# A GRU recurrence inside a graph network: one hand-over of the new state instead of two, gate sums in SBUF instead of PSUM

## The reference, cut to what matters

```python
def step(h, pi):                     # pi: what the input gives to the gates, computed ahead
    ph = h @ W_hh.T + b_hh           # 512 -> 1536
    r = sigmoid(pi[:H] + ph[:H])
    z = sigmoid(pi[H:2*H] + ph[H:2*H])
    n = tanh(pi[2*H:] + r * ph[2*H:])
    h_new = (1.0 - z) * n + z * h
    return h_new, h_new
ys = scan(step, h0, pre_i)           # 1250 steps, each needs the state of the one before
```

## Time and profile before

| | |
|---|---|
| median of 3 runs | 5284.1 us (5284.08 to 5288.26) |
| the profiled execution's own time | 5288.3 us, its span 5286.2 us |
| PE busy | 5071.3 us, 96% of the span |
| PE weight loads | 4262.3 us, 81% |
| DVE, ACT, POOL busy | 57%, 40%, 18% |
| matmuls of the recurrence (L501) | 120000 of 128234 |

### The profile page before, as it was taken

One profiled execution on the slowest core, in us unless ns is written; L12 is line 12 of the kernel. 1 busy time (PEld: TensorE's weight loads), 2 busy tenths in 40 slices (PEclk: granted clock), 3 DMA queues, 4 the chain that ended last, 5 costly groups with the idle time before them and its releaser, 6 DMA issues.

```text
span 5286.2 us, 338777 instructions
## 1 busy us (share of the span) xinstructions
PE 5071.3 (96%) x128234; PEld 4262.3 (81%) x128235; DVE 3006.4 (57%) x16450; ACT 2112.3 (40%) x15422; POOL 943.4 (18%) x5221
## 2 busy tenths in 40 slices
PE   5669999999999999999999999999999999999989
PEld 4555559999999999999999999999999645555654
DVE  6662336666666666666666666666666444355551
ACT  0110005555555555555555555555555201221110
POOL 1230002222222222222222222222222100000000
PEclk8559999999999999999999999999999998999989
DMA  1002220000000000000000000000000100001011
GB/s 59 0 3 97 80 87 0 0 0 0 0 0 0 0 0 0 0 0 0 0 0 0 0 0 0 0 0 0 0 0 0 54 8 10 35 35 35 19 46 45
DMA packets 28930, 81.07 MB, mean 15 GB/s; under 512 B 1594, under 2 KB 1834, under 8 KB 28858
## 3 DMA queue, kind: packets, MB, share of 16 engines
q1 hardware_dynamic: 28858, 80.03, 4.1%
HBM read 58.08 MB, written 21.95 MB: 15 GB/s over the span
## 4 chain that ended last, share of the span: by engine, by line
PE 92%; DVE 3%; issue 3%; DVEq 2%; ACT 0%; POOL 0%; DMA 0%; SPq 0%; POOLq 0%; ACTq 0%
PE psum L501 63%; PE psum L570 8%; PE psum L376 5%; PE psum L366 4%; PE psum L582 4%; PE psum L483 2%; PE psum L556 2%; PE psum L646 1%; PE psum L423 1%; DVE r L879 1%; DVEq L874 1%; DVE r L878 1%; DVEq L872 1%; DVEq L871 1%; PE psum L433 0%
## 5 line engine op out<-in xcount | busy, mean ns | idle before, releaser
L501 PE MATMUL psum<-h,r 128*128 128x16 f16 (+1 forms) x80000 | 3063.4, 181 | 11.1 <-ACT psum L706 4.4
L501 PEld LDWEIGHTS psum<-h,r 128*128 128x128 f16 x80000 | 2544.2, 96 | 113.0 <-ACT psum L706 5.0
L501 PE MATMUL psum<-h,hn 128*128 128x16 f16 (+1 forms) x40000 | 1801.3, 178 | 0.0
L501 PEld LDWEIGHTS psum<-h,hn 128*128 128x128 f16 x40000 | 1416.5, 96 | 0.0
L997 DVE TENSOR_TENSOR_SCAN psum<-mul_rz,psum 128x6 f32<-128x6 f32 x5000 | 871.6, 174 | 611.9 <-PE psum L501 563.1
L706 ACT COPY psum<-big 128x2 f32 (+1 forms) x7506 | 1002.8, 163 | 0.0
L328 POOL TENSOR_TENSOR upd_add<-upd,signs 128x4 f32<-128x4 f32 x2500 | 499.4, 200 | 2708.0 <-DVE h L1014 1524.0
L719 ACT ACTIVATE mul_n<-psum 128x2 f32<-128x2 f32 x2500 | 434.4, 174 | 1197.8 <-DVE psum L997 1197.8
L1011 DVE TENSOR_TENSOR_SCAN upd<-upd_mul,upd_add 128x8 f32<-128x8 f32 x2500 | 437.1, 175 | 414.1 <-ACT upd_mul L724 299.3
L728 ACT ACTIVATE upd_add<-psum 128x2 f32<-128x2 f32 x2500 | 433.4, 173 | 254.3 <-DVE psum L1003 238.7
L1003 DVE TENSOR_TENSOR_SCAN psum<-mul_n,psum 128x8 f32<-128x8 f32 x2500 | 446.8, 179 | 112.6
(11 more groups left out here) (231 smaller groups left out, 2791.2 us busy)
## 6 DMA issues: line engine op xcount, KB each, us to landing
ws<-in_Wl SPq DMA_DIRECT2D x9, 1024.0 KB, 5.3
ws<-in_Wr SPq DMA_DIRECT2D x9, 1024.0 KB, 7.7
edge_counts<-adj SPq DMA_DIRECT2D x2, 3051.8 KB
edge_weights<-big SPq DMA_DIRECT2D x1, 6103.5 KB
adj_rows<-big SPq DMA_DIRECT2D x1, 6103.5 KB
adj<-adj_rows SPq DMA_DIRECT2D x1, 6103.5 KB
big<-edge_counts SPq DMA_DIRECT2D x1, 6103.5 KB
adj<-edge_weights SPq DMA_DIRECT2D x1, 6103.5 KB
```

What stands on the lines that cost most here:

```text
L501: m = mm(places, whh16[g][:, part, 2 * kc + k, (2 * c + j) * P:(2 * c + j + 1) * P], state.unsqueeze(1).broadcast_to([P, COPIES, 2 - part] ...
```

## The change

The diff does these things:

- `high_part` and `low_part` go. The update scan gets 14 columns instead of 8: after the new state (column 2 of each 7) come the state times 4096 (3), the same with `ROUND` added (4), with `ROUND` taken away again (5), which leaves the rounded high part, and a zero (6). One `tensor_tensor` of four columns then writes (low, high) as (column 3 minus 5, column 5 minus 6) into `h16`.
- `gru_state{c}` rises once a step. PE waits once for each half.
- The low weights multiply both parts of the state, so that all 96 matmuls write 32 columns, as pairs; high and low weights alternate for each piece.
- `sum_rz` and `sum_n` lie in SBUF.
- On ACT the put of (c 1, gate n) moves ahead of `gate_z(1)`. The puts of r and n for c 1 share one signal, that of z has a semaphore of its own.
- POOL no longer waits for `gru_state{c}`, only for `gru_upd{c}`.

```diff
+ROUND = 1.5 * 2.0 ** 24
-        h16 = sb("h16", [P, 2, 2, 16], F16)
+        h16 = sb("h16", [P, 2, 2, 2, 2], F16)
-        sum_rz = [[psum[:, 4 * c + g, 8 * COPIES:8 * COPIES + 6] for g in range(2)] for c in range(2)]
-        sum_n = [psum[:, 4 * c + 2, 8 * COPIES:8 * COPIES + 8] for c in range(2)]
+        sum_rz = sb("sum_rz", [P, 2, 2, 6])
+        sum_n = sb("sum_n", [P, 2, 8])
-        upd_mul = sb("upd_mul", [P, 2, 8])      # upd_add, upd likewise
+        upd_mul = sb("upd_mul", [P, 2, 14])
...
                 for j, k in pieces:
                     at = (4 if g == 2 else 3) * j
-                    places = psum[...][:, :, at:at + 2 - part]
-                    state = h16[:, u, kc, 8 * k + 6:8 * k + 8 - part]
-                    m = mm(places, whh16[g][:, part, ...], state.unsqueeze(1).broadcast_to([P, COPIES, 2 - part]), ...)
+                    for part in range(2):
+                        m = mm(psum[...][:, :, at:at + 2], whh16[g][:, part, ...],
+                               h16[:, u, kc, k].unsqueeze(1).broadcast_to([P, COPIES, 2]), ...)
...
-                    pe.wait_ge(s("gru_state0"), 2 * t + 1)
+                    pe.wait_ge(s("gru_state0"), t + 1)
                     pe.wait_ge(s("gru_put0"), t + 1)
-                    gru_gate(u, 0, 0, 0, part=1)
-                    pe.wait_ge(s("gru_state0"), 2 * t + 2)
-                    gru_gate(u, 0, 0, 0, part=0)
-                    for g in (1, 2):
+                    for g in range(3):
                         gru_gate(u, 0, 0, g)
-                    pe.wait_ge(s("gru_put1"), 3 * t + 1)
+                    pe.wait_ge(s("gru_put1"), t + 1)
                     gru_gate(u, 1, 0, 0)
-                    pe.wait_ge(s("gru_put1"), 3 * t + 2)
                     gru_gate(u, 1, 0, 2, every[:2])
-                    pe.wait_ge(s("gru_state1"), 2 * t + 1)
-                    gru_gate(u, 0, 1, 0, part=1)
-                    pe.wait_ge(s("gru_state1"), 2 * t + 2)
-                    gru_gate(u, 0, 1, 0, part=0).then_inc(s("gru_r_mm0"), 1)
+                    pe.wait_ge(s("gru_state1"), t + 1)
+                    gru_gate(u, 0, 1, 0).then_inc(s("gru_r_mm0"), 1)
...
-                    put(t + 1, 1, 0).then_inc(s("gru_put1"), 1)
+                    put(t + 1, 1, 0)
                     gate_n(1)
+                    put(t + 1, 1, 2).then_inc(s("gru_put1"), 1)
                     gate_z(1)
-                    put(t + 1, 1, 2).then_inc(s("gru_put1"), 1)
-                    put(t + 1, 1, 1).then_inc(s("gru_put1"), 1)
+                    put(t + 1, 1, 1).then_inc(s("gru_putz1"), 1)
...
-            def high_part(u, c):
-                v.tensor_tensor_scan(h16[:, 1 - u, c, 0:16:2], upd_mul[:, c], upd_add[:, c], 0.0, ALU.mult, ALU.add).then_inc(s(f"gru_state{c}"), 1)
-            def low_part(t, u, c):
-                dve.wait_ge(s(f"gru_state{c}"), 2 * t + 3)
+            def new_state(t, u, c):
                 dve.wait_ge(s(f"gru_upd{c}"), t + 1)
-                v.tensor_tensor(h16[:, 1 - u, c, 7:16:8], upd[:, 1 - u, c, 3:8:4], h16[:, 1 - u, c, 6:16:8], ALU.subtract).then_inc(s(f"gru_state{c}"), 1)
+                new = sevens(upd[:, 1 - u, c])
+                v.tensor_tensor(h16[:, 1 - u, c], new[:, :, 3:6:2], new[:, :, 5:7], ALU.subtract).then_inc(s(f"gru_state{c}"), 1)
```

More of the change, by code:

```diff
@@ L324, in _ @@
                     for c in range(2):
-                        pool.wait_ge(s(f"gru_state{c}"), 2 * t + 3)
                         pool.wait_ge(s(f"gru_upd{c}"), t + 1)
-                        new, start = (a.rearrange("p (j a) -> p j a", a=4) for a in (upd[:, 1 - u, c], upd_add[:, c]))
+                        new, start = (a.rearrange("p (j a) -> p j a", a=7) for a in (upd[:, 1 - u, c], upd_add[:, c]))
                         pool.tensor_tensor(start[:, :, 1:3], new[:, :, 2:3].broadcast_to([P, 2, 2]), signs[:].rearrange("p (j a) -> p j a", a=2), ALU.mult).then_inc(s(f"gru_fresh{c}"), 1)
-                        pool.tensor_copy(r1[:, 2 * c:2 * c + 2, bass.ds(t, 1)], upd[:, 1 - u, c, 2:8:4]).then_inc(s(f"gru_kept{c}"), 1)
+                        pool.tensor_copy(r1[:, 2 * c:2 * c + 2, bass.ds(t, 1)], upd[:, 1 - u, c, 2:14:7]).then_inc(s(f"gru_kept{c}"), 1)
             def roots(n0, n1):
@@ L490, in _, with gru_gate @@
             every = ((0, 0), (0, 1), (1, 0), (1, 1))
[L492 to L496, removed]
+            def gru_gate(u, c, kc, g, pieces=every):
                 for j, k in pieces:
                     at = (4 if g == 2 else 3) * j
-                    places = psum[:, 4 * c + g, 0:8 * COPIES].rearrange("p (r a) -> p r a", a=8)[:, :, at:at + 2 - part]
-                    state = h16[:, u, kc, 8 * k + 6:8 * k + 8 - part]
-                    m = mm(places, whh16[g][:, part, 2 * kc + k, (2 * c + j) * P:(2 * c + j + 1) * P],
-                           state.unsqueeze(1).broadcast_to([P, COPIES, 2 - part]), start=(kc == 0 and j == 0 and k == 0 and part == 1),
-                           stop=(kc == 1 and k == 1 and part == 0), skip_group_check=True)
+                    for part in range(2):
+                        m = mm(psum[:, 4 * c + g, 0:8 * COPIES].rearrange("p (r a) -> p r a", a=8)[:, :, at:at + 2],
+                               whh16[g][:, part, 2 * kc + k, (2 * c + j) * P:(2 * c + j + 1) * P],
+                               h16[:, u, kc, k].unsqueeze(1).broadcast_to([P, COPIES, 2]), start=(kc == 0 and j == 0 and k == 0 and part == 0),
+                               stop=(kc == 1 and k == 1 and part == 1), skip_group_check=True)
                 return m
@@ L710, in _ @@
             put(0, 0, 2).then_inc(s("gru_put0"), 1)
-            for g in (0, 2, 1):
-                put(0, 1, g).then_inc(s("gru_put1"), 1)
+            put(0, 1, 0)
+            put(0, 1, 2).then_inc(s("gru_put1"), 1)
+            put(0, 1, 1).then_inc(s("gru_putz1"), 1)
             with act.Fori(0, N // 2) as i:
@@ L981, in _ @@
             link(v.memset(upd_mul[:], 1.0))
[L982 to L983 removed]
+            link(v.memset(upd_mul[:, :, 0:14:7], 0.0))
+            link(v.memset(upd_mul[:, :, 3:14:7], HS))
+            link(v.memset(upd_mul[:, :, 6:14:7], 0.0))
             link(v.memset(upd_add[:], 0.0))
+            link(v.memset(upd_add[:, :, 4:14:7], ROUND))
+            link(v.memset(upd_add[:, :, 5:14:7], -ROUND))
             link(v.memset(signs[:], 1.0))
@@ L991, in _, with sevens @@
             for c in range(2):
-                dve.sem_inc(s(f"gru_state{c}"), 2)
+                dve.sem_inc(s(f"gru_state{c}"), 1)
                 dve.sem_inc(s(f"gru_fresh{c}"), 1)
+            def sevens(ap):
+                return ap.rearrange("p (j a) -> p j a", a=7)
             def scan_rz(t, c, g):
                 dve.wait_ge(s(f"gru_{'rz'[g]}_mm{c}"), t + 1)
-                v.tensor_tensor_scan(sum_rz[c][g], mul_rz[:], psum[:, 4 * c + g, 0:6], 0.0, ALU.mult, ALU.add).then_inc(s(f"gru_{'rz'[g]}_sum{c}"), 1)
+                v.tensor_tensor_scan(sum_rz[:, c, g], mul_rz[:], psum[:, 4 * c + g, 0:6], 0.0, ALU.mult, ALU.add).then_inc(s(f"gru_{'rz'[g]}_sum{c}"), 1)
             def scan_n(t, c):
@@ L1002, in scan_n @@
                 dve.wait_ge(s(f"gru_n_mm{c}"), t + 1)
-                v.tensor_tensor_scan(sum_n[c], mul_n[:, c], psum[:, 4 * c + 2, 0:8], 0.0, ALU.mult, ALU.add).then_inc(s(f"gru_n_sum{c}"), 1)
+                v.tensor_tensor_scan(sum_n[:, c], mul_n[:, c], psum[:, 4 * c + 2, 0:8], 0.0, ALU.mult, ALU.add).then_inc(s(f"gru_n_sum{c}"), 1)
             def update(t, u, c):
```

24 lines of the change are left out of this document (12 added, 12 removed).

## The result

The changed kernel takes 5340.5 us (median of 4 runs, 5339.8 to 5343.9) against 5284.4 us: ratio 1.0106, 95% interval 1.0091 to 1.0121. It is slower, as forecast, but by 56 us where 156 were forecast; the time lies 10 us under the low end of the range. Per step of the recurrence the forecast was +121 ns.

A forecast was written before the change was run, and what follows sets the result against it. The prediction took each recurrence step to be bound by the circle of waits from S to S. Terms 40 + 40 + 6 + 30 + 5 = 121 ns, times 1250 = 151 us, on 5288.3 gave 5440 us, range 5350 to 5510.

The forecast's parts named there:

- The circle: Chain of waits in each recurrence step, from S through gate n, scan, tanh, update, state and PE; delays on it count fully.
- S: Point in each step where PE loads the first weights that need the state's half 1.
- The matmul term: PE's r and z gates: four slow column-3 matmuls instead of two, +8 ns per gate, five gates on the circle, +40 ns.
- Handing over the state: Update start to PE going on: longer scan and later subtraction, less the second hold, +40 ns a step.
- The second hold: PE held again for the low part, four slots after going on, in the kernel before; 0.025 us lost a step.
- Sums in SBUF: Gate sums moved from PSUM: scan n writing SBUF +6 ns, tanh reading SBUF +30 ns a step.
- Half 1: Half 1's chain, with a put ahead of sigmoid z, arrives together with S; counted +5 ns a step.
- Nothing: POOL's earlier start, the puts' signals and a few memsets ahead of the loop, all priced at zero.
- Wide writes are free: Rival on PE's matmuls: one slot price for up to 64 columns; +81 ns a step, 5389 us, chance 0.12.
- PE answers late: Rival at the state wait: PE goes on 0.13 instead of 0.05 behind the subtraction; +80, 5540 us, chance 0.07.
- SBUF reads cost nothing: Rival on ACT's tanh and sigmoids: no SBUF price in short instructions; +85 ns a step, 5394 us, chance 0.08.
- the hand-over gets faster: Rival from update to S: one PE wait and one DVE instruction less; at best -10 ns, 5276 us, chance 0.04.

The follow-up runs named there:

- run 3: The changed kernel with the low weights multiplying the high part alone, 16 columns instead of 32: 5337.1 us, ratio 1.0106.
- run 2: The changed kernel with the gate sums back in PSUM: 5316.1 us, ratio 1.0066.
- run 4: The changed kernel with the gate sums in PSUM and narrow low weights (16 columns): 5304.4 us, ratio 1.0035.
- run 12: The kernel before with r and z pairs at columns 0 and 4, PE's put wait first, twelve narrow matmuls ahead of twelve wide ones: 5241.1 us, ratio 0.9929.
- run 11: The kernel before with pairs at columns 0 and 4, low weights multiplying (zero, high part), so all 96 matmuls write aligned pairs: 5180.3 us, ratio 0.981.
- run 6: The kernel before with the pairs of gates r and z at columns 0 and 4 instead of 0 and 3: 5230.0 us, ratio 0.9902.
- run 7: The changed kernel with the pairs of gates r and z at columns 0 and 4: 5281.0 us, ratio 0.9996.
- run 9: The changed kernel with pairs at columns 0 and 4 and half 1's gate n put behind sigmoid z again: 5236.3 us, ratio 0.9915.
- run 13: The changed kernel with the state's semaphore counted in twos, so a register instruction stands between PE's state and put waits: 5554.2 us, ratio 1.0506.
- run 5: The kernel before with PE waiting once for each half, for the low part too: 5492.7 us, ratio 1.0397.
- run 1: The kernel before with the gate sums in SBUF as its only change: 5306.5 us, ratio 1.0044.
- run 10: The kernel before with PE's wait for the put written ahead of its wait for the high part: 5322.3 us, ratio 1.0088.

## Where the prediction held and where it failed

- **The circle** was right: S, gate n, scan n, tanh, update, state, PE. In the changed kernel no term outside it cost anything, and every edit on it told. The direction was right for the reason given, a longer circle; of the 68 ns between the forecast's 121 and the measured 53, the matmuls are some 30 to 34, the hand-over 20, the sums 12 to 15, half 1 the 5.
- **The matmul term (+40 ns) is the step that failed.** It measured 6 ns (run 3) to 10 (runs 2 and 4). "96 stay 96 ... 16 columns more are free there" was half of it. The part foreseen came: four slow pairs a gate, 29.2 instead of 25.0. But I put the widening itself at nothing, from the durations of single matmuls (177 and 178 ns), and took a slot of 26 as given. The slots tell another thing: 16 single columns have one of 26.0 to 26.7, 16 aligned pairs 25.0 (run 12). Over the 60 matmuls on the circle, 30 of them narrow before, this is 0.7 each in the mean (the slow ones too fall, from 29.3 and 30.5 to 29.2), 42 ns, and that pays for the slow pairs. Run 3 takes both away and little moves; run 11 takes the slow pairs away and has no narrow ones, and both gains stand (50 us below run 6); runs 6 and 7/9 show the slow pairs' price, 42 and 83 ns. That the price lies in where a pair begins was right too.
- **Handing over the state (+40) measured +20.** The working from the update to PE, 0.445, measured 0.441. The base was off: the one step I read had 0.38, the mean is 0.40 (steps of the kernel before lie between 2654 and 2737 ns, which one step can't show; those after between 2734 and 2743). What makes it so cheap: the state is complete 0.13 us later behind the update's start than the high part was (254 to 384 ns), and PE answers in 57 ns where it took 146. The second hold, some 20 ns, goes as well. The prediction used both answers rightly, with the reason left at "one wait right at a matmul's weights"; run 13 bears it out with 74 ns, run 5 with the other sign. The 146 are a mean of two kinds of step: 130 in the second step of each turn of the loop, and 136 to 190 in the first one, where PE's branch and the loop's register instructions come shortly before (the last of them ends on average 165 ns ahead of the first matmul). That is also the unevenness of the steps, 2663 and 2709 in turn; it is read from the trace and no run tests it.
- **Sums in SBUF (+36) measured +21 to +24** (runs 1 and 2, and the table). Tanh +33 for +30; scan n -8 or -9 for +6. Of the two pairs of rows at hand I chose the wrong one: copies of two columns, where the scans' own pair (175 all in SBUF, 179 all in PSUM) had the sign right.
- **Half 1 (+5)** was 0: slack at S is about 30 ns. The place was right, though: with the slow pairs gone the put ahead of sigmoid z makes it the bound (run 7 against run 9, 45 us).
- **The puts** stood under *Nothing*, with a look only at the one for (c 1, n), which does come early. The one that a step's start waits for, (c 0, n), ends 0.05 behind the high part; it cost the forecast nothing, but run 10 shows what it costs to lean on it.
- **Rivals.** "Wide writes are free" came nearest by its number, 5389, for a wrong reason: where they begin at column 3 they aren't free (runs 6, 7), they were paid for. Its +81 are 28 ns above the measured 53, and these lie in the other terms (hand-over 20, sums 12 to 15, half 1 5, less the 6 to 10 that the matmuls did cost). No rival on the slower side reached as low as what happened, since each changed one term, and all came out small at once; the low end of the range should have held the terms' low bounds together. "PE answers late", "SBUF reads cost nothing" and "the hand-over gets faster" are refuted by the rows.

One sentence of the Trainium skill, that 1 to 64 columns cost the same ("TensorE: Matmul & The Clock Gate", Back-to-back issue gap), holds here only for aligned pairs: its floor of about 25 ns is the slot of 25.0 seen in run 11. The measurements decide for the others: 26.0 to 26.7 for 16 single columns (run 12), 29.2 for 16 pairs from column 3.

**Open.** Why 16 single columns have a longer slot than 16 pairs isn't settled; no run separates what is written from what is read, since both change together. That a pair at column 3 and 32 single places cost alike fits a count of separate 16-byte pieces (columns 3 and 4 lie in two, 0 and 1 in one), 32 against 16; but 16 single columns are 16 pieces too and not as fast as 16 pairs, so the count isn't all, and only these layouts were tried. Why the stage ahead of the loop moves by some us between kernels, and why the granted clock at the loop's start differs, wasn't followed up.

## What to carry to other kernels

In a stream of small matmuls, compare layouts by the time from start to start over many of them, not by how long one takes: here the narrower output had the longer slot. Writing all of them as pairs that lie within one aligned group of four was worth 2% of the whole kernel, more than any of the three ideas of the change. Price a term on a recurrence's circle with the mean over hundreds of steps, not with the one step that is read; and put no term at nothing because two durations agree. Before a wait is moved or merged, look whether it ends up on the instruction that needs it or on a register instruction ahead of it.

## What the runs showed of the hardware

- PE's start to start for 128x128 fp16 weights: 25.0 ns for 16 pairs of fp32 columns at column 0 or 4 of 8, 26.0 to 26.7 for 16 single columns (12 in a row, run 12), 25.6 to 25.8 in the mean of both, 29.2 to 30.5 for 16 pairs that begin at column 3, and 28 to 30 for 32 single columns 8 apart.
- PE takes up a wait at its weights 0.05 to 0.06 us behind the release; where the wait is on a register instruction ahead of them it is 0.13 (runs 5, 10 and 13), and up to 0.19 behind the loop's branch (kernel before).
- A tanh or sigmoid of two columns takes 173 ns from PSUM and 197 to 207 from SBUF; a scan of 8 columns 179 into PSUM and 170 into SBUF.
- A DVE instruction that raises its semaphore by 2 took 189 ns where one that raises it by 1 took 164.
